# Order of the on-chip buffers: the matrix operands of a transformer block begin at one place modulo 512 bytes

## The chip, the core and the metric

The kernel runs on one core of a Trainium2 chip. The metric is device time in microseconds (us) of one execution; less is better. The engines are named as in the profile: PE is the tensor engine (its weight loads have a row kind of their own, PEld), DVE the vector engine, ACT the scalar engine, POOL the general-purpose engine, SP the engine that here issues all transfers.

## What is computed

The input x has 8 sequences of 2048 tokens with 256 channels, in float32. After a plain layer norm of each token the block below is applied; its attention is linear (one 256x256 matrix of keys and values per sequence), and its output is gated by a second branch with ternary weights.

```python
xn = _layernorm(x)
q, k, v = split(xn @ Wqkv + bqkv)
qp, kp = elu(q) + 1, elu(k) + 1
kv  = einsum('bsd,bse->bde', kp, v)
num = einsum('bsd,bde->bse', qp, kv)
den = einsum('bsd,bd->bs', qp, sum_s(kp))
y   = layer_norm(xn + num / (den + 1e-6), g1, b1)
ffn = (silu(y @ Wg + bg) * (y @ Wu + bu)) @ Wd + bd          # hidden width 682
s   = layer_norm(y + ffn, g2, b2)
g   = silu(xn @ (ternary(weight) * scale).T)
out = x + s * g
```

## The kernel before

The 16384 tokens are 32 groups of 512. One iteration of the steady loop works on several groups at once: keys (K) and the key-times-input sums (XK) of the group five ahead, queries (Q) two ahead, attention (N) and the ternary branch (B) one ahead, and the feed-forward (G, U, GU, D) of the current one. A group's tokens come in four tiles of 128. Once per sequence of four groups the two KV jobs turn the sums into the matrix kv. What each engine does, and in which order, is written out by hand in tables (`TENSOR_JOBS`, `VECTOR_STEPS`, `SCALAR_STEPS`, `GPSIMD_STEPS`); the engines run in program order and wait for one another by semaphores. Four more tables serve the start and the end.

Nearly every product on PE is made of two numbers that are each split into a high and a low part of type float32r, so that a product takes three matmuls, high*high, low*high and high*low (`parts3`). The left operand of a pair is the stationary one (128 columns, loaded before the matmul), the right one is the moving one, 512, 258 or 256 columns wide. All matmuls of the steady loop are issued at line 1271:

```python
def products(dst, pairs, name, first=True, last=True, **kw):
    for n, (left, right) in enumerate(pairs):
        ins = eng.matmul(dst, left, right, start=first and n == 0, ...)
```

In the names of the profile the moving operand stands ahead of the stationary one: `bank<-zT_h,wgu_h` moves zT_h through loaded wgu_h (jobs G, U, GU, 66 matmuls in an iteration), `d_bank<-wd_h,h_h` moves the weights wd_h through the loaded hidden rows h_h (D, 64). The others are `xT,wq` (Q, 12), `wk,xT` (K, 24), `kp_h,xn_h` into `xk_bank` (XK, 24), `kv,qp` (N, 24) and `tern,xT` (B, 16): 230 matmuls in an iteration without KV jobs, 246 with them. A weight load of the next matmul runs while the current one streams.

Results leave PSUM over ACT and DVE. For each of the five full blocks of the hidden layer DVE's `h_rows` (line 1095, `bank<-bank,hb,hs`) takes what ACT's `silu_gate` (`hs<-bank,hb`) made, ACT's `h_high` (`h_h<-bank`) rounds it to the high part, and DVE's `h_low` (line 1105, `h_l`) makes the low part, for which job D waits. ACT's activations all stand at line 695. Five PSUM banks go round as a ring among the jobs (`freed` says what a job waits for before it takes the next bank).

The tensors in SBUF are allocated one after the other in the order of the `sb(...)` calls, each rounded up to 32 bytes, behind 16512 bytes that are taken already; so the order of the calls and the shapes give each one's address. `SHIFT = 8` makes the rows of kv_h, kv_l, qp_h and qp_l 32 bytes longer than 1024 or 2048 bytes, so that their second half (the second 128 of 256 channels) begins 32 bytes further on modulo 512. All other steps within an operand tensor (a tile, a block of 128 columns, a slot of a ring) are multiples of 512 bytes.

Of the kernel before, what the change touches and what calls it, by code (L numbers as in the profile page):

```python
# [30 lines left out]
P = 128  # L31
D = 256
DC = D // P
# [3 lines left out]
HC = HF + 1  # L37
# [7 lines left out]
TILES = TOK // P  # L45
# [6 lines left out]
SHIFT = 8  # L52
# [9 lines left out]
LN0 = LEAD + 1  # L62
# [150 lines left out]
def build_kernel(nc, x, wqkv, bqkv, wg, bg, wu, bu, wd, bd, g1, b1, g2, b2, wt, out):  # L213
    f32, f32r = mybir.dt.float32, mybir.dt.float32r
# [9 lines left out]
    with ctx:  # L224
        def sb(name, shape, dt=f32):
            return ctx.enter_context(nc.sbuf_tensor(name, shape, dt))
# [2 lines left out]
            return ctx.enter_context(nc.semaphore(name))  # L229


        ident = sb("ident", [P, P])
        consts = sb("consts", [P, 4])
        masks = sb("masks", [P, 2])
        norm1 = sb("norm1", [P, 2, TILES])
        norm2 = sb("norm2", [P, 2, TILES])
        kp_h = sb("kp_h", [P, TILES, D], f32r)
        kp_l = sb("kp_l", [P, TILES, D], f32r)
        den = sb("den", [P, 2, 2])
        wd_h = sb("wd_h", [P, HC, D], f32r)  # L240
        wd_l = sb("wd_l", [P, HF, D], f32r)
        kv_h = sb("kv_h", [P, DC, D + SHIFT], f32r)
        hb = sb("hb", [P, 2 * HC])
        hb0 = sb("hb0", [P, 2 * HC])
        hb1 = sb("hb1", [P, 2 * HC])
        kv_l = sb("kv_l", [P, DC, D + SHIFT], f32r)
        ve = sb("ve", [P, 3, TILES])
        vecs = sb("vecs", [P, 5, DC])
        rstd0 = sb("rstd0", [P, LN0, TILES])
        wk_h = sb("wk_h", [P, DC, D], f32r)  # L250
        wk_l = sb("wk_l", [P, DC, D], f32r)
        tern = sb("tern", [P, DC, D], f32r)
        wq_h = sb("wq_h", [P, DC, D], f32r)
        wq_l = sb("wq_l", [P, DC, D], f32r)
        tscale = sb("tscale", [P, 4])
        xT_h = sb("xT_h", [P, XT, DC, TOK], f32r)
        xT_l = sb("xT_l", [P, XT, DC, TOK], f32r)
        h_h = sb("h_h", [P, HRING, TOK], f32r)
# [8 lines left out]
        NGU = (2 * HF + 1) * P  # L267
        wgu_h = sb("wgu_h", [P, DC, NGU], f32r)
        wgu_l = sb("wgu_l", [P, DC, NGU], f32r)
        qp_h = sb("qp_h", [P, DC, TOK + SHIFT], f32r)  # L270
        nmr0 = sb("nmr0", [P, LN0, TILES])
        mv = sb("mv", [P, 3, TILES, 2])
        qp_l = sb("qp_l", [P, DC, TOK + SHIFT], f32r)
        st = sb("st", [P, 3, TILES, 6])
        bvb = sb("bvb", [P, D])
        bk1b = sb("bk1b", [P, D])
        g1b = sb("g1b", [P, D])
# [1202 lines left out]
```

## Time and profile before

| | |
|---|---|
| median of three executions | 1211.84 us (1211.64 to 1212.23) |
| the profiled execution, first to last instruction | 1210.2 us |
| PE busy | 1190.8 us, 98% |
| PE weight loads busy | 1069.3 us, 88% |
| DVE busy | 1081.9 us, 89% |
| ACT busy | 953.3 us, 79% |
| POOL busy | 842.7 us, 70% |
| granted TensorE clock | 0.998 of full over the span |

The profiled execution has no time of its own beside its span; the span is 1.6 us under the median of the timed ones. A matmul's record lasts longer than the distance to the next matmul's start, since the records overlap; so busy time of PE says that it always had something in hand, and not at what pace. Of two matmuls of one width with records of different length, the longer one is followed by a later start.

### The profile page before, as it was taken

How to read it: one execution, taken by the hardware profiler on the slowest of the kernel's cores; microseconds unless marked ns; L12 is line 12 of the kernel's file. 1: busy time of each engine (PE TensorE's matmuls, PEld its weight loads, DVE VectorE, ACT ScalarE, POOL GpSimd, SP SyncE). 2: the span in 40 equal slices, each digit the busy share in tenths (PEclk: the TensorE clock that was granted, in tenths of full speed). 3: DMA queues.
4: the chain of work that ended last, by engine and by line, in shares of the span. 5: the costliest groups of instructions: out<-in, count | busy, mean ns of one | idle time of the engine just before them, and what ended most of it. 6: DMA issues, size and time to landing. Idle time of an engine off the chain costs nothing.

```text
span 1210.2 us, 24021 instructions
## 1 busy us (share of the span) xinstructions
PE 1190.8 (98%) x7550; PEld 1069.3 (88%) x7550; DVE 1081.9 (89%) x2467; ACT 953.3 (79%) x1557; POOL 842.7 (70%) x994
## 2 busy tenths in 40 slices
PE   8999999999999999999999999999999999999997
PEld 6889998999988999988999988889988999888896
DVE  6988999999999999999999999999999999777765
ACT  7787888878888878888878887778887878867753
POOL 3443786767787776777767777667876777766676
PEclk9999999999999999999999999999999999999999
DMA  7313432334432334432334332244432343222201
GB/s 201 91 49 88 123 106 70 88 105 123 123 102 72 89 106 123 119 104 74 88 106 122 115 104 74 77 122 123 115 93 60 101 123 105 70 71 61 76 22 35
DMA packets 137523, 115.61 MB, mean 96 GB/s; under 512 B 12339, under 2 KB 122293, under 8 KB 137398
## 3 DMA queue, kind: packets, MB, share of 16 engines
q1 hardware_dynamic: 137398, 114.08, 32.6%
q8 instruction: 62, 1.02, 0.4%
q14 instruction: 63, 0.52, 0.1%
HBM read 67.38 MB, written 46.67 MB: 94 GB/s over the span
## 4 chain that ended last, share of the span: by engine, by line
PE 90%; DVE 5%; issue 2%; DMA 2%; ACT 1%; POOL 1%; SPq 0%; DVEq 0%; POOLq 0%; ACTq 0%
PE bank L1271 63%; PE d_bank L1271 18%; PE xk_bank L1271 8%; DVE st L922 1%; DMA xa<-z_turned 1%; DMA z_turned<-xa 1%; PE bank L1285 1%; DVE rz L1054 0%; DVE zT_l L1085 0%; POOL norm L569 0%; DVE bank L1095 0%; ACT rz L695 0%; DVE xn L974 0%; DVE mv L929 0%; DVE h_l L1105 0%
## 5 line engine op out<-in xcount | busy, mean ns | idle before, releaser
L1271 PE MATMUL bank<-zT_h,wgu_h 128*128 128x512 f32 x704 | 275.6, 391 | 0.8 <-DVE rz L1054 0.7
L1271 PE MATMUL bank<-zT_l,wgu_h 128*128 128x512 f32 x704 | 275.7, 392 | 0.0
L1271 PE MATMUL bank<-zT_h,wgu_l 128*128 128x512 f32 x704 | 275.4, 391 | 0.0
L695 ACT ACTIVATE rz<-rz,norm 128x256 f32<-128x256 f32 x252 | 140.5, 595 | 56.2 <-DVE norm L1131 55.6
L569 POOL TENSOR_TENSOR norm<-ve,consts 128x4 f32<-128x4 f32 x64 | 72.9, 1139 | 153.6 <-DVE ve L933 153.4
L1271 PE MATMUL d_bank<-wd_h,h_h 128*128 128x256 f32 x640 | 179.1, 280 | 0.1
L1271 PE MATMUL d_bank<-wd_h,h_l 128*128 128x256 f32 x640 | 178.9, 279 | 0.0
L1271 PE MATMUL d_bank<-wd_l,h_h 128*128 128x256 f32 x640 | 178.8, 279 | 0.0
L1095 DVE SCALAR_TENSOR_TENSOR bank<-bank,hb,hs 128x512 f32<-128x512 f32 x160 | 117.9, 754 | 53.1 <-ACT hs L695 41.4
L695 ACT ACTIVATE h_h<-bank 128x512 fp32r<-128x512 f32 x160 | 95.8, 599 | 80.8 <-DVE bank L1095 80.4
L1271 PEld LDWEIGHTS bank<-zT_l,wgu_h 128*128 128x128 f32 x704 | 132.1, 188 | 28.8
L1271 PEld LDWEIGHTS bank<-zT_h,wgu_h 128*128 128x128 f32 x704 | 132.7, 189 | 25.4 <-DVE rz L1054 3.2
L695 ACT ACT_TABLE_LOAD x116 | 148.8, 1283 | 4.0 <-POOL wd_l L678 1.2
L1271 PEld LDWEIGHTS bank<-zT_h,wgu_l 128*128 128x128 f32 x704 | 132.1, 188 | 20.6
L695 ACT ACTIVATE hs<-bank,hb 128x512 f32<-128x512 f32 x192 | 128.2, 685 | 16.2 <-PE bank L1271 15.1
L592 POOL TENSOR_TENSOR ksum<-ksum,kp 128x256 f32<-128x256 f32 x120 | 108.1, 901 | 47.0 <-DVE kp L1021 43.6
L1105 DVE TENSOR_TENSOR h_l<-bank,h_h 128x512 fp32r<-128x512 f32 x160 | 110.0, 687 | 23.4 <-ACT h_h L695 17.5
L1271 PEld LDWEIGHTS d_bank<-wd_h,h_h 128*128 128x128 f32 x640 | 120.2, 188 | 3.1 <-DVE h_l L1105 0.5
L1271 PEld LDWEIGHTS d_bank<-wd_h,h_l 128*128 128x128 f32 x640 | 120.2, 188 | 2.8
L1271 PEld LDWEIGHTS d_bank<-wd_l,h_h 128*128 128x128 f32 x640 | 121.9, 190 | 0.0
L642 POOL TENSOR_TENSOR rz<-rz,g1b 128x256 f32<-128x256 f32 x128 | 117.9, 932 | 0.0
L602 POOL TENSOR_TENSOR rz<-rz,g2b 128x256 f32<-128x256 f32 x124 | 90.6, 741 | 35.0 <-ACT rz L695 35.0
(163 smaller groups left out, 3576.2 us busy)
## 6 DMA issues: line engine op xcount, KB each, us to landing
xq<-in_L_attn_x_dram SPq DMA_DIRECT2D x32, 512.0 KB, 5.9
xa<-in_L_attn_x_dram SPq DMA_DIRECT2D x31, 512.0 KB, 3.9
out_dram<-rz SPq DMA_DIRECT2D x31, 512.0 KB, 5.0
z_turned<-xa SPq DMA_DIRECT2D x120, 128.0 KB, 3.3
xa<-z_turned SPq DMA_DIRECT2D x30, 512.0 KB, 4.1
turned<-xa SPq DMA_DIRECT2D x108, 128.0 KB, 2.5
xa<-turned SPq DMA_DIRECT2D x27, 512.0 KB, 3.9
rz<-in_L_attn_Wg_dram SPq DMA_DIRECT2D x1, 640.0 KB, 7.4
```

Of the source, the lines that this page charges most:

```text
L569: eng.tensor_tensor(dst, ve[:, k, :], neg_half[:, 0:1].to_broadcast([P, TILES]), ALU.pow).then_inc(S[f"rs{k}"], 1)
L592: eng.tensor_tensor(ksum[:, slot, :], ksum[:, slot, :], part, ALU.add).then_inc(S["ks"], 1)
L602: eng.tensor_tensor(row_, row_, g2b[:, :], ALU.mult).then_inc(S["a"], 1)
L642: eng.tensor_tensor(row_, row_, g1b[:, :], ALU.mult).then_inc(S["zg"], 1)
L695: return eng.activation(out_, in_, func, **kw).then_inc(S[name], 1)
L922: eng.bn_stats(st[:, k, t, :], rows).then_inc(S[f"bn{k}"], 1)
L1095: eng.scalar_tensor_tensor(out=hidden(g, c)[0:rows, :], in0=up, scalar=hb[0:rows, HC + c:HC + c + 1], in1=hs[0:rows, n % 2, :], op0=ALU.ad ...
L1105: eng.tensor_tensor(h_l[:, slot, :], hidden(g, c)[:, :], h_h[:, slot, :].bitcast(f32), ALU.subtract).then_inc(S["hl"], 1)
L1271: ins = eng.matmul(dst, left, right, start=first and n == 0, stop=last and n == len(pairs) - 1, **kw)
L1285: ins = eng.transpose(dst[:, c * D + t * P:c * D + (t + 1) * P], src[:, 2 * p + t, c * P:(c + 1) * P], ident[:, :])
```

## The change

Only the order of the `sb(...)` calls changes, and a tensor `spare` of 32 bytes, which nothing uses, is added. The instructions of each engine, their order and their waits are the same.

```diff
-        ident = sb("ident", [P, P])
         consts = sb("consts", [P, 4])
         masks = sb("masks", [P, 2])
         norm1 = sb("norm1", [P, 2, TILES])
         norm2 = sb("norm2", [P, 2, TILES])
+        den = sb("den", [P, 2, 2])
+        hb = sb("hb", [P, 2 * HC])
         kp_h = sb("kp_h", [P, TILES, D], f32r)
         kp_l = sb("kp_l", [P, TILES, D], f32r)
-        den = sb("den", [P, 2, 2])
         wd_h = sb("wd_h", [P, HC, D], f32r)
         wd_l = sb("wd_l", [P, HF, D], f32r)
-        kv_h = sb("kv_h", [P, DC, D + SHIFT], f32r)
-        hb = sb("hb", [P, 2 * HC])
-        hb0 = sb("hb0", [P, 2 * HC])
-        hb1 = sb("hb1", [P, 2 * HC])
-        kv_l = sb("kv_l", [P, DC, D + SHIFT], f32r)
...
         wgu_l = sb("wgu_l", [P, DC, NGU], f32r)
+        kv_h = sb("kv_h", [P, DC, D + SHIFT], f32r)
+        st = sb("st", [P, 3, TILES, 6])
+        mv = sb("mv", [P, 3, TILES, 2])
+        hb0 = sb("hb0", [P, 2 * HC])
         qp_h = sb("qp_h", [P, DC, TOK + SHIFT], f32r)
...
+        spare = sb("spare", [P, 8])
+        kv_l = sb("kv_l", [P, DC, D + SHIFT], f32r)
         qp_l = sb("qp_l", [P, DC, TOK + SHIFT], f32r)
+        ident = sb("ident", [P, P])
```

Added up from the shapes, the matrix operands begin at these places (address modulo 512 bytes):

| tensors | role | before | after |
|---|---|---|---|
| zT_h, zT_l; wgu_h, wgu_l | moving; stationary | 352; 352 | 352; 352 |
| xT_h, xT_l | moving in Q, stationary in K and B | 352 | 352 |
| wq_h, wq_l | stationary | 320 | 352 |
| wk_h, wk_l, tern | moving | 320 | 352 |
| wd_h, wd_l | moving | 288 | 352 |
| h_h, h_l, ht | stationary | 352 | 352 |
| kp_h, kp_l | moving | 256 | 352 |
| xn_h, xn_l | stationary | 352 | 352 |
| kv_h; kv_l | moving in N | 288; 32 | 352; 352 |
| qp_h; qp_l | stationary in N | 352; 96 | 352; 416 |

qp_l alone is not at the common place: behind kv_l, which is 2112 bytes long, it begins 64 bytes further on. The float32 buffers that ACT, DVE, POOL and the transfers work on (xa, xn, kp, ku, xq, qp, rz, sg, hs) all move by 32 bytes, from 448 to 480.

## Rows read from the trace of the kernel before

**Rows 1.** The page: busy time of the engines, and shares of the chain that ended last.

```profile
PE 1190.8 (98%) x7550; PEld 1069.3 (88%) x7550; DVE 1081.9 (89%) x2467; ACT 953.3 (79%) x1557; POOL 842.7 (70%) x994
PE 90%; DVE 5%; issue 2%; DMA 2%; ACT 1%; POOL 1%; SPq 0%; DVEq 0%; POOLq 0%; ACTq 0%
```

**Rows 2.** Groups of PE by form, whole span: count | busy us, mean ns | idle before.

```profile
L1271 PE MATMUL bank<-zT_l,wgu_h 128*128 128x512 f32 x704 | 275.7, 392 | 0.0
L1271 PE MATMUL bank<-xT_l,wq_h 128*128 128x512 f32 x128 | 50.6, 395 | 0.0
L1271 PE MATMUL d_bank<-wd_h,h_l 128*128 128x256 f32 x640 | 178.9, 279 | 0.0
L1271 PE MATMUL bank<-wk_h,xT_l 128*128 128x256 f32 x256 | 72.1, 282 | 0.0
L1271 PE MATMUL xk_bank<-kp_l,xn_h 128*128 128x256 f32 x224 | 62.9, 281 | 0.0
L1271 PE MATMUL bank<-kv_l,qp_h 128*128 128x258 f32 x256 | 72.8, 285 | 0.0
```

**Rows 3.** Groups of PE by form, 482.0 to 485.7 us.

```profile
L1271 PE MATMUL bank<-zT_l,wgu_h 128*128 128x512 f32 x6 | 2.3, 389 | 0.0
```

**Rows 4.** Groups of PE by form, 602.3 to 604.2 us.

```profile
L1271 PE MATMUL d_bank<-wd_h,h_l 128*128 128x256 f32 x6 | 1.7, 276 | 0.0
```

**Rows 5.** Chain that ended last: start us, us, work; pieces of three iterations.

```profile
109.41 18.63 PE bank L1271 x106
...
145.25 18.63 PE bank L1271 x106
...
601.49 2.74 PE d_bank L1271 x24
604.23 2.73 PE bank L1271 x12
...
609.07 2.13 PE xk_bank L1271 x18
...
612.57 2.83 PE d_bank L1271 x24
615.40 1.42 PE bank L1271 x12
```

**Rows 6.** Busy time by stretch: us, then each engine's busy time (count), clock, DMA.

```profile
20.00:75.00 55.00, 51.77 (x326) 42.72 (x325) 47.64 (x116) 44.19 (x76) 26.62 (x28) 1.00 0.35 97
200.00:600.00 400.00, 400.00 (x2568) 362.22 (x2568) 375.59 (x849) 330.19 (x536) 298.24 (x343) 1.00 0.35 102
1085.00:1210.00 125.00, 115.67 (x706) 102.66 (x705) 85.89 (x203) 70.54 (x121) 80.54 (x100) 0.98 0.19 58
```

**Rows 7.** Waits from 200 to 1000 us: us in total, times, longest us.

```profile
DVE bank L1095 <- ACT hs L695: 27.2, 22, 1.7
PEld bank L1271 <- DVE h_l L1105: 3.3, 11, 0.3
ACT hs L695 <- PE bank L1271: 2.3, 9, 0.5
DVE rz L1117 <- PE d_bank L1271: 0.3, 1, 0.3
```

**Rows 8.** Timeline of ACT and DVE: start us, us, work, [idle before <- releaser].

```profile
631.11 0.60 ACT L695 ACTIVATE h_h<-bank 128x512 fp32r<-128x512 f32 x1 [1.78 <-DVE bank L1095]
...
647.38 1.26 ACT L695 ACTIVATE hs<-bank,hb 128x512 f32<-128x512 f32 x2
...
648.16 1.42 DVE L1095 SCALAR_TENSOR_TENSOR bank<-bank,hb,hs 128x512 f32<-128x512 f32 x2 [1.17 <-ACT hs L695]
...
666.02 0.74 DVE L1095 SCALAR_TENSOR_TENSOR bank<-bank,hb,hs 128x512 f32<-128x512 f32 x1
...
666.79 0.60 ACT L695 ACTIVATE h_h<-bank 128x512 fp32r<-128x512 f32 x1 [1.77 <-DVE bank L1095]
...
739.09 0.60 ACT L695 ACTIVATE h_h<-bank 128x512 fp32r<-128x512 f32 x1 [1.78 <-DVE bank L1095]
```

More of the change, by code:

```diff
@@ L236, in build_kernel @@
         norm2 = sb("norm2", [P, 2, TILES])
+        den = sb("den", [P, 2, 2])
+        hb = sb("hb", [P, 2 * HC])
         kp_h = sb("kp_h", [P, TILES, D], f32r)
         kp_l = sb("kp_l", [P, TILES, D], f32r)
-        den = sb("den", [P, 2, 2])
         wd_h = sb("wd_h", [P, HC, D], f32r)
         wd_l = sb("wd_l", [P, HF, D], f32r)
-        kv_h = sb("kv_h", [P, DC, D + SHIFT], f32r)
-        hb = sb("hb", [P, 2 * HC])
-        hb0 = sb("hb0", [P, 2 * HC])
-        hb1 = sb("hb1", [P, 2 * HC])
-        kv_l = sb("kv_l", [P, DC, D + SHIFT], f32r)
-        ve = sb("ve", [P, 3, TILES])
-        vecs = sb("vecs", [P, 5, DC])
-        rstd0 = sb("rstd0", [P, LN0, TILES])
         wk_h = sb("wk_h", [P, DC, D], f32r)
@@ L254, in build_kernel @@
         wq_l = sb("wq_l", [P, DC, D], f32r)
-        tscale = sb("tscale", [P, 4])
         xT_h = sb("xT_h", [P, XT, DC, TOK], f32r)
@@ L269, in build_kernel @@
         wgu_l = sb("wgu_l", [P, DC, NGU], f32r)
+        kv_h = sb("kv_h", [P, DC, D + SHIFT], f32r)
+        st = sb("st", [P, 3, TILES, 6])
+        mv = sb("mv", [P, 3, TILES, 2])
+        hb0 = sb("hb0", [P, 2 * HC])
         qp_h = sb("qp_h", [P, DC, TOK + SHIFT], f32r)
         nmr0 = sb("nmr0", [P, LN0, TILES])
-        mv = sb("mv", [P, 3, TILES, 2])
+        rstd0 = sb("rstd0", [P, LN0, TILES])
+        vecs = sb("vecs", [P, 5, DC])
+        ve = sb("ve", [P, 3, TILES])
+        hb1 = sb("hb1", [P, 2 * HC])
+        tscale = sb("tscale", [P, 4])
+        spare = sb("spare", [P, 8])
+        kv_l = sb("kv_l", [P, DC, D + SHIFT], f32r)
         qp_l = sb("qp_l", [P, DC, TOK + SHIFT], f32r)
-        st = sb("st", [P, 3, TILES, 6])
+        ident = sb("ident", [P, P])
         bvb = sb("bvb", [P, D])
```

## The prediction

> **What bounds the kernel now.** I read the page first, then the groups of PE, then the chain and the waits. By the page PE is the bound: 98% busy, and 90% of the chain that ended last is its work [rows 1]; between 200 and 600 us it is busy without a gap, with DVE at 94% of that stretch [rows 6]. But PE's busy time hides its pace, so I took the pace from the chain, which lists runs of back-to-back matmuls. 24 matmuls of D took 2.74 us and 24 others, in the same iteration and from the same tensors, 2.83: 114.2 and 117.9 ns from start to start. 12 of G and U took 2.73 (227.5 ns), 18 of XK 2.13 and 12 of K 1.42 (118.3 each) [rows 5]. The record of a matmul lasts some 162 ns longer than its distance to the next: 389 against 227.5 in a quiet stretch of the 512-wide ones [rows 3], 276 against 114 in the quick run of D [rows 4]. So the mean records over the span give the mean distances: 512-wide 392 in G and U and 395 in Q, 256-wide 279 in D, 281 in XK, 282 in K, and 285 for the 258-wide of N [rows 2]. The shortest lengths that the kernel shows are 389 and 276.
>
> Set beside the places of the operands: G and U, with both at 352, get to 389 and their mean is 3 ns over it. Q (352 against 320) is 6 over it. Every 256-wide form has unequal places (32 to 96 bytes apart, N more), and its mean is 3 to 6 ns over 276, N's 9.
>
> Then I asked whether PE sets the time in the steady loop at all. Its own iteration, where it hardly waits, is 35.84 us: the long run of 106 starts at 109.41 and again at 145.25 [rows 5]. Beside it runs a ring that PE has no part in. ACT's h_high starts at 631.11, ACT works on to the silu_gate pair at 647.38, for which DVE waits 1.17 us; DVE works on from 648.16 to the h_rows at 666.02, for which ACT waits, and h_high starts again at 666.79: one round, 35.68 us. The same row comes again, two rounds later, at 739.09, so that three rounds took 107.98 us, 35.99 each [rows 8]. That is more than PE's own 35.84. From 200 to 1000 us DVE waited 27.2 us for this silu, in each of 22 iterations, and for PE only 0.3; ACT's silu waited 2.3 for PE, and PE's weight loads waited 3.3 for h_low in 11 iterations [rows 7]. So the ring of ACT and DVE and the stream of PE are level, and the ring is a shade the longer one. What is taken from PE's matmuls in the steady loop comes back as a wait of PE for h_low or for a bank.
>
> **The change, part by part.** No instruction, wait or transfer is moved; only what PE's reads meet can change. Pricing each form by its shortest record gives an upper estimate of what PE's stream gets back:
> - G, U, GU: places unchanged, 2112 matmuls, 3 ns over 389 in the form shown, the other two forms a little less; I take 5 us, if nothing ahead of them disturbs them any more.
> - Q: 384 x 6 ns = 2.3 us. D: 2048 x 3 ns = 6.1. K: 768 x 6 = 4.6. XK: 672 x 5 = 3.4. B, priced as K (its row is not shown, 5 ns): 512 x 5 = 2.6.
> - N: 768 x 8 ns (9, less one for two more columns) = 6.1 at most; qp_l stays 64 bytes off and the second halves follow 32 bytes further, so I take half, 3.
>
> Together 27 us over 7264 matmuls, 3.7 ns each, 0.85 us in an iteration of 230. For the 256-wide forms the trace has no float32r pair at equal places. The gain there lies between nothing (the mean rows of today) and 276 ns; the nearest row is G and U, which sit at 389 at equal places, and D reaches 276 at unequal ones, so the stream can run at that pace. I take 276.
>
> One written rule says that the places don't matter at all: the Trainium skill ("TensorE: Matmul & The Clock Gate", Step-by-step: what each phase is for) says that the moving operand and the weight load have independent read ports into SBUF and that loading the next weights takes no read bandwidth from the running matmul. By that rule the 27 us are 0; it doesn't explain the 6 ns between Q and the quiet stretch of G and U.
>
> Now what of the 27 us arrives at the end:
> - Start, 20 to 75 us: 326 matmuls, PE busy 51.8 of 55, DVE 47.6 [rows 6]. 326 x 3.7 ns = 1.2 us, all of it on the path.
> - Steady loop, some 28 iterations: the ring allows only what it itself waits for PE, 2.3 + 0.3 us in 22 iterations [rows 7], 0.12 each, 3.3 us in all. A wait taken away there often shows the next one behind it; I take a little under half, 1.5 us.
> - End, from 1085 us: 706 matmuls, 2.6 us, but PE is without work for 9.3 of 125 us there [rows 6], so that the chain passes through other engines; half, 1.3 us.
>
> Sum 4.0 us: the profiled 1210.2 becomes 1206.2, and with the 1.6 us between the profiled execution and the median of the timed ones, **1207.8 us**, 0.33% less. Bounds of this case: 1.2 + 3.3 + 2.6 = 7.1 us off (1204.7) if every allowance is used; 1.5 us off (1210.3) if only G, U and Q gain, 7 of the 27 us. ACT, DVE and POOL and the transfers also get their buffers 32 bytes further on; I cost that at nothing: kp_l, zT_l and h_low read pairs of buffers at several places and nothing in the rows sets them apart. If it cost DVE 1 ns of an instruction, the ring's some 76 in a round would add 2 us over the span.
>
> **The rivals.**
> - The places don't matter; what comes ahead does. For it: D ran at 114.2 and at 117.9 ns at the very same places in one iteration [rows 5], so something beside the place decides. Against it: the two 512-wide forms differ all the way. It gives 0 of 27 us, 1211.8. Chance 0.24.
> - PE is the bound after all and the 27 us arrive in full: for it speak 98% and 90% [rows 1]; against it the three rounds of 35.99 against 35.84. 1211.8 - 27 = 1185. Chance 0.05.
> - Slower: the two reads meet at the start. If a weight load begins together with the matmul that it runs beside, then at equal places both begin in the same spot (no row here tells whether that costs anything). In a 512-wide matmul there is time left behind the load, in a 256-wide one there is not, and equal places are shown here for 512-wide alone. Price: the 152 matmuls of 256 or 258 columns of an iteration go from a mean record of about 280 to that of the dearest form, 285 [rows 2]: +0.76 us, less 0.23 for G, U and Q, gives PE's own iteration 36.37 against the ring's 35.99; 0.38 x 31 = 12 us, 1224. It decides from where PE's iteration passes the ring's, 0.15 us (and the 0.23) over 152 matmuls: 2.5 ns each. Chance 0.09.
> - The forecast case has the remaining 0.62, in 0.05 of which the gain is under 0.2%.
>
> **How the numbers follow.** A measurement of this kernel tells changes over about 0.2% (2.4 us) from none. Faster: 0.57 of the forecast case and 0.05 for the full gain, 0.62. Same: 0.24 and 0.05, 0.29. Slower: 0.09. The range takes the forecast case from 1203.8 (its bound of 1204.7 and the spread between executions) and the case without effect up to 1212.4; the full gain and the slower case are left out, 0.14. The forecast case's own range is 1204.7 to 1210.3.
>
> **What would show it.** Mean records over the span: 389 to 390 in G, U and Q, 276 to 277 in D, K, XK and B, some 280 in N; runs of 24 in D at 2.72 us, both of them. Then PE's own iteration is near 35.0, but ACT's h_high still comes at 35.7 to 36.1 us, DVE's wait for the silu stays near 1.2 us in each iteration, and PE shows new waits of some 0.8 us in an iteration, for h_low (L1105) or for a bank that DVE frees. If the records of 256-wide matmuls stay at 279 to 282, the step on places is wrong; if they shorten and h_high comes every 35.0 us, the step on the ring is wrong; if they lengthen to 283 or more, the slower rival is right. The forecast is also wrong where ACT's or DVE's own instructions change in length.

## The result, and the profile after

The changed kernel takes 1216.38 us in the median of 4 executions (1215.35 to 1218.28), the kernel before 1211.74 beside it (1211.23 to 1212.23). The ratio is 1.0041, 95% interval 1.003 to 1.0053: slower by 0.41%, 4.6 us. Forecast was 1207.8. The profiled execution of the changed kernel was the slowest of its four, 1218.28; its span lies 6.4 us above the one of before, and not 4.6.

The page of the changed kernel, busy times and the chain's shares:

```profile
PE 1197.7 (98%) x7550; PEld 1079.4 (89%) x7550; DVE 1081.8 (89%) x2467; ACT 953.4 (78%) x1557; POOL 842.5 (69%) x994
PE 85%; DVE 7%; issue 3%; ACT 2%; DMA 2%; POOL 1%; SPq 0%; DVEq 0%; ACTq 0%; POOLq 0%
```

Against [rows 1] only PE and its weight loads have more busy time, 6.9 and 10.1 us. DVE, ACT and POOL are within 0.2 us of before, so their buffers' 32 bytes cost them nothing. The chain runs less through PE (85% for 90%) and more through DVE.

PE's groups by form, whole span (count | busy us, mean ns | idle):

```profile
L1272 PE MATMUL bank<-zT_h,wgu_h 128*128 128x512 f32 x704 | 276.6, 393 | 0.8 <-DVE rz L1055 0.7
L1272 PE MATMUL bank<-zT_h,wgu_l 128*128 128x512 f32 x704 | 276.0, 392 | 0.0
L1272 PE MATMUL bank<-zT_l,wgu_h 128*128 128x512 f32 x704 | 274.1, 389 | 0.0
L1272 PE MATMUL d_bank<-wd_h,h_l 128*128 128x256 f32 x640 | 181.1, 283 | 0.0
L1272 PE MATMUL bank<-wk_h,xT_l 128*128 128x256 f32 x256 | 72.9, 285 | 0.0
L1272 PE MATMUL bank<-tern,xT_l 128*128 128x256 f32 x256 | 64.1, 283 | 0.0
L1272 PE MATMUL xk_bank<-kp_l,xn_h 128*128 128x256 f32 x224 | 63.4, 283 | 0.0
L1272 PE MATMUL bank<-kv_l,qp_h 128*128 128x258 f32 x256 | 72.3, 282 | 0.0
L1272 PE MATMUL bank<-xT_l,wq_h 128*128 128x512 f32 x128 | 49.9, 390 | 0.0
```

Beside [rows 2] the two widths part. Q, 512 wide and new at equal places, got shorter: from 395 to 390. What is 256 wide got longer: D from 279 to 283, K from 282 to 285, XK from 281 to 283. Among the narrow ones only N is shorter; its form shown went from 285 to 282, its other two went from 285 both to 285 and 284. G, U and GU, whose places did not change, gained nothing as a whole. The form zT_l went from 392 to 389, but the two others went up, as the rows of the kernel before show:

```profile
L1271 PE MATMUL bank<-zT_h,wgu_h 128*128 128x512 f32 x704 | 275.6, 391 | 0.8 <-DVE rz L1054 0.7
L1271 PE MATMUL bank<-zT_h,wgu_l 128*128 128x512 f32 x704 | 275.4, 391 | 0.0
```

With the 275.7 us of [rows 2] the three forms are busy for 826.7 us before, and 826.7 after.

The chain that ended last, pieces (start us, us, work):

```profile
110.04 18.54 PE bank L1272 x106
146.07 18.54 PE bank L1272 x106
...
203.08 2.87 PE d_bank L1272 x24
...
214.34 2.87 PE d_bank L1272 x24
```

Both runs of 24 in D now take 2.87 us, 119.6 ns from start to start, where they took 2.74 and 2.83 [rows 5]. The long run of 106, which holds Q and part of G and U, is 0.09 us shorter. PE's own iteration went from 35.84 us to 146.07 - 110.04 = 36.03. That is what the forms add up to, each by the change of its distance as the starts give it: D 64 x 3.3 ns, K 24 x 1.5, XK and B 40 x 0.75, N 24 x -0.7, Q 12 x -5.2, together +0.2 us; the 66 of G, U and GU keep their 229 ns.

The start of the ring of ACT and DVE (start us, us, work, [idle before <- releaser]), and the waits from 200 to 1000 us (us in total, times, longest us):

```profile
634.98 0.60 ACT L696 ACTIVATE h_h<-bank 128x512 fp32r<-128x512 f32 x1 [1.78 <-DVE bank L1096]
```

```profile
DVE bank L1096 <- ACT hs L696: 27.1, 22, 1.6
ACT hs L696 <- PE bank L1272: 6.7, 21, 0.6
```

h_high comes again at 671.24, 707.43 and 743.46: 36.16 us a round, where three rounds of before gave 35.99 [rows 8]. So 0.17 us more in each of some 28 iterations, 4.8 us. Over 22 rounds, from the h_high at 229.18 (after: 230.87) on, it is 801.74 us before and 805.32 after, 0.16 each. The ring has not become longer by itself: its silu now waits for PE 6.7 us in 21 iterations, where it waited 2.3 in 9 [rows 7]. PE's own 36.03 us stand above the 35.99 of the three rounds of before.

### The profile page after: what moved, and what is told of

It reads as the page before. It is cut to its first block, busy times and chain, and to the rows that moved or that the text cites. A ratio compares the mean times of both kernels' runs of the same rounds, so it can differ in the third digit from the quotient of the medians.

```text
span 1216.6 us, 24021 instructions
## 1 busy us (share of the span) xinstructions
PE 1197.7 (98%) x7550; PEld 1079.4 (89%) x7550; DVE 1081.8 (89%) x2467; ACT 953.4 (78%) x1557; POOL 842.5 (69%) x994
## 4 chain that ended last, share of the span: by engine, by line
PE 85%; DVE 7%; issue 3%; ACT 2%; DMA 2%; POOL 1%; SPq 0%; DVEq 0%; ACTq 0%; POOLq 0%
PE bank L1272 60%; PE d_bank L1272 18%; PE xk_bank L1272 7%; DVE st L923 1%; DMA z_turned<-xa 1%; DVE rz L1055 1%; DMA xa<-z_turned 1%; PE bank L1286 1%; DVE bank L1096 1%; DVE h_l L1106 1%; DVE zT_l L1086 1%; ACT rz L696 0%; POOL norm L570 0%; ACT h_h L696 0%; DVE rz L1118 0%
```

## The experiments

Three of them move single operands, four measure the place by itself, one tests the ring, and two look for the best order. Every kernel of the block itself was timed beside the kernel before, whose median was 1211.93, 1211.26 and 1211.43 us in the three sittings.

**1. All places for 256-wide matmuls, in steps of 32 bytes.** Theory P: the distance between the starts depends on the place of the moving operand beside that of the stationary one. Rival O: it doesn't. The core of the kernel, with stat the stationary tensor and moving the sixteen tensors ma to mp, each 32 bytes further behind it:

```python
for m in moving:
    for n in range(6):    # 512 wide, at equal places
        eng.matmul(bank[0], stat[block n % 4], wide, ...)
    for n in range(48):
        eng.matmul(bank[1][:, 0:256], stat[block n % 4], m, ...)
```

> A kernel of its own that computes nothing of the reference: 16 runs of 48 float32r matmuls, 256 columns wide, one loaded 128-column operand of a ring of four after the other, the moving operand beginning 0, 32, 64, ... 480 bytes behind the stationary ones modulo 512 (tensors ma, mb, ... mp), with six 512-wide matmuls at equal places ahead of each run. Theory P (the place of the moving operand against the stationary one sets the pace, equal places are the dear ones): ma settles at 120 ns from start to start, as the 256-wide matmuls of the changed kernel do; other places lie between 113 and 119, and those that the kernel before had (moving 64 bytes ahead, 32 ahead, 96 ahead: mo, mp, mn) near 118. Rival O (something else of the new order, not the place, lengthens them): all 16 runs show one pace within 1 ns.

Timeline of PE, the runs of 48 (start us, us, work). A matmul's distance to the next is the run's time less its last record, 0.28 us, over 47:

```profile
16.63 5.76 PE L54 MATMUL bank<-mb,stat 128*128 128x256 f32 x48
23.62 5.82 PE L54 MATMUL bank<-mc,stat 128*128 128x256 f32 x48
30.66 5.92 PE L54 MATMUL bank<-md,stat 128*128 128x256 f32 x48
37.79 5.92 PE L54 MATMUL bank<-me,stat 128*128 128x256 f32 x48
44.94 5.86 PE L54 MATMUL bank<-mf,stat 128*128 128x256 f32 x48
...
66.10 5.90 PE L54 MATMUL bank<-mi,stat 128*128 128x256 f32 x48
73.22 5.76 PE L54 MATMUL bank<-mj,stat 128*128 128x256 f32 x48
```

At 32 bytes (mb) the runs settle at 116.7 ns, at 64 at 117.8, at 96 and 128 at 120.0, at 160 at 118.8. From 256 bytes on (mi) the same numbers come again, to the tenth of a ns: the period is 256 bytes, not 512. At equal places (ma; mi in the fence, the same place in this period) a matmul takes 120.0 ns, the dearest value of the sweep. P holds and O falls. Not expected was that 96 and 128 bytes are as dear as 0. The stationary tensor stands at 128 modulo 512 in this kernel and at 352 in the block. A moving operand at 128 takes 120.0 ns here, beside a stationary one at 128, and 116.8 in experiment 7, beside ones at 352: it is the distance between the two that counts, and not the moving operand's own place.

**2 to 4. One operand pair alone.** Experiment 2 is the kernel before with the moving operands of D at the place of their stationary ones; experiment 3 is the changed kernel with those of D 64 bytes under, as before; experiment 4 is the kernel before with Q at equal places.

```diff
 # e2, kernel before: wd_h and wd_l begin at 352
-        wd_h = sb("wd_h", [P, HC, D], f32r)
-        wd_l = sb("wd_l", [P, HF, D], f32r)
...
+        wd_h = sb("wd_h", [P, HC, D], f32r)
+        wd_l = sb("wd_l", [P, HF, D], f32r)
         xT_h = sb("xT_h", ...)
 # e3, changed kernel: the same two lines ahead of hb, at 288
 # e4, kernel before: wq_h and wq_l ahead of xT_h, at 352
```

> The kernel before with wd_h and wd_l alone moved, so that D has both operands at place 352; all other tensors keep their places. Theory P: D's mean record goes from 279 to 283, 3.3 ns for each of 2048 matmuls or 6.7 us of PE, PE's own iteration from 35.84 to 36.05, and the kernel is 4 to 6 us slower (1216 to 1218). Rival O: D stays at 279 and the time at 1211.8.

> The changed kernel with wd_h and wd_l alone put back to place 288, 64 bytes under h_h and h_l. Theory P: D's mean record comes back to 279 to 281, and the time to 1211 to 1213, most of the 4.6 us, since D has 64 of the 152 256-wide matmuls of an iteration and the largest part of what they lost. Rival O: the time stays at 1216.

> The kernel before with wq_h and wq_l alone moved to place 352, that of xT. Theory P says for the 512-wide form that equal places are the cheap ones: Q's mean record goes from 395 to 390, 2 us of PE over the span, of which the ring of ACT and DVE leaves 0 to 1 us in the time: 1210.8 to 1211.8. Rival O: Q stays at 395.

| kernel | median us | ratio to before (95%) |
|---|---|---|
| e2, before, D at equal places | 1216.66 | 1.0036 (1.0024 to 1.0049) |
| e3, changed, D 64 bytes under | 1213.7 | 1.0015 (1.0006 to 1.0024) |
| e4, before, Q at equal places | 1211.8 | 0.9993 (0.9984 to 1.0002) |

Groups by form, of e2 and then of e3:

```profile
L1271 PE MATMUL d_bank<-wd_l,h_h 128*128 128x256 f32 x640 | 180.9, 283 | 0.0
```

```profile
L1272 PE MATMUL d_bank<-wd_h,h_l 128*128 128x256 f32 x640 | 179.4, 280 | 0.0
```

D in e3, from the chain (start us, us, work):

```profile
202.33 2.83 PE d_bank L1272 x24
...
213.52 2.83 PE d_bank L1272 x24
...
217.78 1.83 PE d_bank L1272 x16
```

The group of Q in e4 (ns min/median/max, first and last start):

```profile
L1271 PE MATMUL bank<-xT_l,wq_h x128: 388/389/398, 18.7 to 1134.5; 128*128 128x512 f32 x128
```

D alone, 2048 of the 7550 matmuls, makes the kernel before 4.7 us slower, as much as the whole change does. Put back in the changed kernel it returns 2.7 of 4.6 us, to 1213.7, above the 1211 to 1213 that were expected. Its two runs of 24 are both at 2.83 us there though the operands lie as before; the quick pace has moved to its third run, 16 matmuls in 1.83 us (114.4 ns), which mostly take 1.88 in the kernel before. That does not explain the 1.8 us that are still missing: PE's own iteration is down to 35.80 us in e3 (long runs start at 511.73, 547.53 and 583.33), under the 35.84 of before. What holds this kernel back is open; the profiled execution, 1212.47 us, is the fastest of its eleven, so the trace may not show it. In e4 Q's median record is the shortest one, 389 where it was 396, which takes some 2 us out of PE's stream. The time does not move by more than its interval, which reaches from 1.9 us less to 0.2 more, so this one alone doesn't tell whether the 2 us arrive.

**5. All places for 512-wide matmuls**, the same kernel with the full width and 24 matmuls at each place.

> The kernel of the first sweep (it computes nothing of the reference) with runs of 24 matmuls of 512 columns in place of 48 of 256. Theory P, with what the first sweep showed (the pace repeats every 256 bytes, equal places 120 ns, 32 bytes behind 116.7): the 512-wide form goes the other way, ma and mi (0 and 256 bytes) settle at 226.7 ns, all others between 230 and 236. Rival: the order of the places is the same for both widths, and ma is the slowest here too.

Groups by form of this kernel, at 32, 64 and 256 bytes:

```profile
L54 PE MATMUL bank<-mb,stat 128*128 128x512 f32 x24 | 5.8, 395 | 0.0
L54 PE MATMUL bank<-mc,stat 128*128 128x512 f32 x24 | 5.7, 391 | 0.0
L54 PE MATMUL bank<-mi,stat 128*128 128x512 f32 x24 | 5.6, 389 | 0.0
```

At equal places, and 256 bytes apart, a matmul takes 226.7 ns; 64 bytes apart 228.9; at every other step of 32 bytes 233.3 to 234.3. Only the value at 64 bytes lies outside what theory P gave. So equal places are the cheapest of these steps for 512 columns and, by experiment 1, the dearest for 256, together with 96 and 128 bytes. The best place for 256 (32 bytes behind) is a dear one for 512.

**6. 256-wide in steps of 4 bytes**, from 0 to 60: the moving operand is a slice `m[:, k:k+256]`. It asks whether places count in pieces of 32 bytes.

> The first sweep with steps of 4 bytes in place of 32 (the moving operand begins 0, 4, ... 60 bytes behind the stationary one; nothing of the reference is computed). Theory P with a place that is read in pieces of 32 bytes or more: 0 to 28 bytes all at 120, 32 to 60 all at 116.7. Rival: the pace goes over smoothly, or has its best place at a distance that is no multiple of 32, below 116 ns; 113.3 ns, which D reached in some of its runs in the kernel before, would be such a place.

Timeline of PE, the runs of 48 at 8, 12, 28, 32 and 36 bytes:

```profile
25.84 6.20 PE L54 MATMUL bank<-mc,stat 128*128 128x256 f32 x48
33.27 5.76 PE L54 MATMUL bank<-md,stat 128*128 128x256 f32 x48
...
61.70 5.71 PE L54 MATMUL bank<-mh,stat 128*128 128x256 f32 x48
68.64 5.77 PE L54 MATMUL bank<-mi,stat 128*128 128x256 f32 x48
75.62 5.98 PE L54 MATMUL bank<-mj,stat 128*128 128x256 f32 x48
```

Every 4 bytes count: 126.7 ns at 8 bytes, 116.7 at 12, 115.5 at 28 (the best of the two sweeps), 116.7 at 32, 121.2 at 36. There are no pieces of 32 bytes, as theory P had it, and the best place of the sweep is at no multiple of 32, as the rival said; but the pace doesn't go over smoothly, and I found no rule behind the sixteen values.

**7. The best place of the sweep put to use.** The kernel before with kp, wd, wk and tern (seven tensors) ahead of consts, at 128: 288 bytes behind the stationary ones, which is 32 in a period of 256. wq goes to 352 as in e4.

```diff
+        kp_h, kp_l, wd_h, wd_l, wk_h, wk_l, tern = ...   # moved here
         consts = sb("consts", [P, 4])
```

> The kernel before with wd, wk, tern and kp (the moving operands of D, K, B and XK) at place 128, which is 288 bytes behind the stationary ones and by the first sweep's period of 256 the same as 32 behind (116.7 ns), and wq at 352 (equal, for the 512-wide Q). Theory P on PE: mean records 279 in D, K, B and XK, where they were 279 to 282, and 390 in Q; some 5 us less of PE's stream than before. Theory R (the ring of ACT and DVE paces the steady loop): of these at most 1.5 us arrive, 1210.3 to 1211.8. Rival (PE paces it): 1206.8.

Groups by form of this kernel:

```profile
L1271 PE MATMUL d_bank<-wd_h,h_l 128*128 128x256 f32 x640 | 178.4, 279 | 0.0
L1271 PE MATMUL bank<-tern,xT_l 128*128 128x256 f32 x256 | 62.6, 278 | 0.0
L1271 PE MATMUL xk_bank<-kp_l,xn_h 128*128 128x256 f32 x224 | 62.5, 279 | 0.0
```

1208.86 us (1207.69 to 1211.6), ratio 0.9983 (0.9974 to 0.9992): 2.4 us under before and 7.5 under the changed kernel, the fastest full version here, though the interval reaches into what I called no change (0.2%). The mean records are as expected, the time is not: 2.4 us arrive where theory R allowed 1.5, and the rival had put all 5. PE's own iteration is 35.65 us here (109.46 to 145.11 in the chain), and experiment 8 gives the ring's, 35.70: a gain on PE can arrive as far down as that, some 0.14 us in an iteration without KV jobs. D is no better than before: both its runs of 24 take some 2.8 us, in place of one of 2.74 and one of 2.83.

**8. The ring.** The kernel before, with the third matmul of each K product (wk_l by xT_h) left out: 256 matmuls of 118.3 ns, 30 us of PE's stream, and nothing of ACT or DVE. If PE sets the time, 30 us arrive; if the ring does, only what it waits for PE.

```diff
-    parts3(xh, xl, wk_h[:, c, :], wk_l[:, c, :])
+    parts3(xh, xl, wk_h[:, c, :], wk_l[:, c, :])[0:2]
```

> The kernel before without the third of the three matmuls of each product in job K (the low part of wk is left out): 8 matmuls of 118 ns less in an iteration, 0.94 us, and 30 us less over the span, about what the prediction wanted to take from PE's stream. Theory R: PE's own iteration goes to 34.9, the ring stays at 35.7 to 36.0, PE waits for h_low or for banks some 0.8 us more in each iteration, and the time falls by 4 to 8 us only, to 1204 to 1208. Rival (PE paces the loop, and the ring shortens with it): 1182 to 1188.

Waits of this kernel from 200 to 1000 us, and four starts of its ring, one round apart:

```profile
PEld bank L1271 <- DVE rz L1054: 14.6, 22, 1.1
PE bank L1271 <- DVE rz L1054: 6.8, 16, 0.7
PEld bank L1271 <- DVE h_l L1105: 6.6, 21, 0.6
DVE bank L1095 <- ACT hs L695: 26.6, 22, 1.5
```

```profile
918.09 0.60 ACT L695 ACTIVATE h_h<-bank 128x512 fp32r<-128x512 f32 x1 [1.78 <-DVE bank L1095]
...
953.79 0.60 ACT L695 ACTIVATE h_h<-bank 128x512 fp32r<-128x512 f32 x1 [1.77 <-DVE bank L1095]
...
989.49 0.60 ACT L695 ACTIVATE h_h<-bank 128x512 fp32r<-128x512 f32 x1 [1.78 <-DVE bank L1095]
...
1025.19 0.60 ACT L695 ACTIVATE h_h<-bank 128x512 fp32r<-128x512 f32 x1 [1.77 <-DVE bank L1095]
```

1205.56 us, ratio 0.9954 (0.9939 to 0.9969): 5.7 of 30 us arrive, as theory R had it. The three rounds are of 35.70 us each, and of the 17 rounds without KV jobs among the 22 from 227 us on, 13 lie within 0.03 us of that; so 35.70 is what the ring of ACT and DVE needs when PE does not hold it up. The kernel before has seven rounds of 35.68 to 35.71 in the same stretch, and most others without KV jobs lie between 35.8 and 36.4. PE has the time and spends it waiting for banks that DVE frees, and DVE waits for the silu as it did.

**9. What ran before.** Why does D have two paces at one place [rows 5], and why didn't the quick one return in e3? Sixteen runs of 24 256-wide matmuls at D's old place, 64 bytes under the stationary tensor. Ahead of each stand 8 256-wide ones 32 bytes under, and then one 512-wide one at equal places ahead of the first run, two ahead of the second, and so on to sixteen.

> The sweep's kernel (nothing of the reference is computed) with 16 runs of 24 256-wide matmuls at one and the same place, 64 bytes under the stationary operand as D in the kernel before. Ahead of each run stand 8 256-wide ones 32 bytes under it (tensor under, the place of B and K before) and then 1, 2, ... 16 512-wide ones at equal places. Theory S (in D's old place the stream has two lasting paces, 113.3 and 117.8 ns, and what ran before chooses): the runs after few 512-wide ones, 6 among them (ma to about mf), include ones at 113.3, the mean record 276; those behind 9 or more are at 117.8, the mean record 280. Rival: all 16 runs are at 117.8, and the 113.3 of the kernel comes from something else there (the operands' blocks, the waits of the job).

Timeline of PE, the runs behind 2 to 6 wide ones:

```profile
15.72 2.89 PE L58 MATMUL bank<-mb,stat 128*128 128x256 f32 x24
20.09 2.90 PE L58 MATMUL bank<-mc,stat 128*128 128x256 f32 x24
24.70 2.99 PE L58 MATMUL bank<-md,stat 128*128 128x256 f32 x24
29.62 2.99 PE L58 MATMUL bank<-me,stat 128*128 128x256 f32 x24
34.79 2.90 PE L58 MATMUL bank<-mf,stat 128*128 128x256 f32 x24
```

Same places, same widths, and two lasting paces: 113.3 ns behind 1, 2, 3 and 6 wide matmuls, 117.8 behind 4, 5 and all from 7 on. Within a run the pace doesn't change over. So what ran ahead chooses between the paces of a place; in e3 moving other operands moved the quick pace from one run of D to another. The 4.5 ns between the two paces are more than the 3.3 between the places of experiment 1, and the sweeps ran each place behind one history only: another place may have a second pace that they do not show. That D is dear at equal places does not hang on this: it runs at 119 to 120 ns in the changed kernel and in e2, and at 114 or 117.8 in the kernel before.

**10. The rest of the change.** The changed kernel with the same seven tensors at 128. Against experiment 7 it keeps what the change did to the other buffers and to N; if that costs something, it shows here.

```diff
+        kp_h, kp_l, wd_h, wd_l, wk_h, wk_l, tern = ...   # moved here, changed kernel
         consts = sb("consts", [P, 4])
```

> The changed kernel with wd, wk, tern and kp alone moved to place 128, 288 bytes behind the stationary ones (116.7 ns in the first sweep); Q, N and all other buffers as in the changed kernel. Theory P (the 256-wide forms at equal places are the whole loss): mean records 279 in D, K, B and XK, and the time as that of the kernel before with the same four moved (0.9983 of before), 1208 to 1210.5. Rival O (the other buffers' 32 bytes or N's places cost something): 1213 or more.

1210.62 us (1207.74 to 1212.45), ratio 0.9988 (0.9979 to 0.9997). With 32 bytes (modulo 256) between the operands the changed kernel is 5.8 us faster and a shade under before, 0.1 us above what theory P gave. So taking D, K, B and XK off their equal places gives back the whole loss, and rival O falls. The remaining order may cost the 1.8 us to experiment 7, but the two intervals overlap, so that is not shown.

## Why the prediction was wrong

**The step that failed is the price of equal places for the 256-wide forms, "I take 276".** It should have taken 3 ns off D's distances; they grew by 3.3: by 1.7 over the slow run of before and by 5.4 over the quick one. In the changed kernel D's mean record is 283, and the sweep gives 120.0 ns for equal places, beside the 119.6 of D's runs of 24. I had written that the trace has no 256-wide pair at equal places, and then took my value from the nearest row by place (G and U, 389), across the width. The width was what decided. The other support, that D reaches 276 at unequal places, spoke in truth for unequal ones: 113.3 ns is a pace of that place 64 bytes under, after some histories, and it is lost at equal places.

**The slower rival named the right forms and the right direction, with too high a price.** It had said that "equal places are shown here for 512-wide alone", and the records of D, K, XK and B did come to 283 or more in the forms shown, the mark set for it. I priced all 152 narrow matmuls at 5 ns, PE's iteration 36.37; D took 3.3, K 1.5, XK and B under 1, N gained, and the iteration became 36.03. With a chance of 0.09 it was too little: the rows that had me write "between nothing (the mean rows of today) and 276 ns" gave no reason to leave the other side out of the middle value. Its mechanism is not shown: why one place for both costs the narrow matmul time and saves it in the wide one is open, and that the reads "meet at the start" was my argument and stays one. It can't be the whole, since 96 and 128 bytes apart cost as much as 0.

**The rival that places don't matter** falls by experiments 1, 5 and 6: 226.7 to 234.3 ns for 512 columns, 115.5 to 126.7 for 256. The rule of the Trainium skill ("TensorE: Matmul & The Clock Gate", Step-by-step: what each phase is for), independent read ports and no bandwidth taken from the running matmul, does not agree with these numbers for float32r: the place of the moving operand beside the loaded one changes the pace of one width by up to 11.2 ns. Which of the two reads gives way, no run here shows. The rival's other half, that what comes ahead decides, is true beside the place: experiment 9 shows the history at a fixed place to be worth 4.5 ns.

**Q** was priced right: 6 ns; its mean fell by 5, its median by 7. **G, U and GU were not.** I took 5 us "if nothing ahead of them disturbs them any more", and got none: 826.7 us busy before and after. One form went to 389, the other two rose to 392 and 393. No row had said that matmuls whose places stay would shorten when others around them move.

**The step on the ring held for what it forbids, and its reading of the two loops was the wrong way round.** Experiment 8 takes out what the 27 us of the forecast were in size, and 5.7 of 30 arrive. But I had taken 35.99, the mean of three rounds of 35.68, 36.02 and 36.27 us, for the ring by itself, 0.15 us over PE's 35.84. The same three rounds of experiment 8 take 35.72, 36.05 and 35.70 (from 628.15 us on): the third had been held up by PE, the second is long in both, and the ring's own time is 35.70. So outside the iterations with KV jobs PE's stream was the longer loop, by 0.14 us. That fits both signs: a gain on PE arrives until PE's iteration is down to 35.70 (2.4 us in experiment 7) and is swallowed below that, and a loss on PE is paid nearly in full, 0.17 of PE's 0.19 us in each iteration, where 35.99 for the ring would have let 0.04 through, some 1 us over the span. The fit is not complete, as e3 shows: 35.80 us for PE's iteration, and 1.8 us slower than before.

**Start and end** were sized on the same wrong sign. From 20 to 75 us the start shows no gain, 324 matmuls for 326. Some of that may be of this one execution, whose granted clock was 0.50 of full speed from 9.8 to 13.0 us, where it was 1.00 in the kernel before:

```profile
20.00:75.00 55.00, 51.77 (x324) 42.71 (x323) 47.55 (x116) 44.10 (x76) 26.54 (x28) 1.00 0.35 97
200.00:600.00 400.00, 399.95 (x2555) 362.94 (x2554) 373.40 (x836) 327.39 (x532) 294.88 (x340) 1.00 0.35 102
```

These are PE, PEld, DVE, ACT and POOL in two stretches of the changed kernel, for [rows 6]. In the steady stretch PE is as busy as before and gets 13 matmuls fewer done, 0.5%; the busy share tells nothing of the pace.

**Nothing for ACT, DVE and POOL** was right: 1081.8, 953.4 and 842.5 us busy.

## What to carry to other kernels

Where the stationary and the moving operand lie beside each other in SBUF was worth 3% of a float32r matmul's pace here in steps of 32 bytes and up to 10% in steps of 4, and in steps of 32 equal places were the best for 512 columns and among the worst for 256: sweep the place for each width in a small kernel of its own, and never carry a place from one width to the other. Read the pace from runs in the chain or from starts, not from busy time, and expect a neighbour's pace to move too, since a place can have two. When PE's loop is level with another ring to 0.2 us, a gain on PE beyond that is swallowed and a loss is paid, so an uncertain edit there is a bad bet even at even odds. And take a ring's own time from its shortest rounds that come again and again, not from a mean over a few, which here held a wait for the other loop.

## What the runs showed of the hardware

- The pace of float32r matmuls at the full clock depends on the distance of the two operands modulo 256 bytes: 256 columns at 0 and at 256 bytes 120.0 ns both, at 32 and 288 bytes 116.7 both, the latter also in experiment 7 with the operands at other addresses (116.8).
- It depends on it in steps of 4 bytes: 126.7 ns at 8 bytes, 116.7 at 12, 115.5 at 28.
- With 512 columns equal places give 226.7 ns, 64 bytes 228.9, the others 233.3 to 234.3; with 256 columns equal places give 120.0, others 115.5 to 126.7.
- At one place and width there can be two lasting paces, 113.3 and 117.8 ns, and what ran ahead chooses between them: behind 1, 2, 3 and 6 wide ones 113.3, behind 4, 5 and 7 to 16 of them 117.8. What in it chooses stays open, as does the rule behind the 4-byte steps.
